# f and g of the next image projected one chunk sooner, F1's moves behind the scores that read it, and another order of V, first tiles and maxima in the prologue

## What is computed

```python
x = x + attention(group_norm(x), Wq, Wk, Wv, gamma)
# attention, with xf of shape (4, 256, 4096):
f = einsum('qc,bcn->bqn', Wq, xf)        # 64 rows
g = einsum('qc,bcn->bqn', Wk, xf)        # 64 rows
h = einsum('vc,bcn->bvn', Wv, xf)        # 256 rows
scores = einsum('bqn,bqm->bnm', f, g)    # 4096 x 4096
beta = softmax(scores, axis=1)           # over n
out = gamma[0] * einsum('bvn,bnm->bvm', h, beta) + xf
```

## Time and profile before

| | |
|---|---|
| median of 3 runs | 1994.29 us |
| the profiled execution: time | 1999.4 us |
| its span, first to last instruction | 1997.6 us |
| mean granted clock of TensorE | 0.987 |
| TensorE busy | 1904.3 us, 95% |
| VectorE busy | 1591.1 us, 80% |
| ScalarE busy | 1574.7 us, 79% |
| GpSimd busy | 1315.6 us, 66% |

### The profile page before, as it was taken

One profiled execution on the slowest core, in us unless ns is written; L12 is line 12 of the kernel. 1 busy time (PEld: TensorE's weight loads), 2 busy tenths in 40 slices (PEclk: granted clock), 3 DMA queues, 4 the chain that ended last, 5 costly groups with the idle time before them and its releaser, 6 DMA issues. The chain is left out here.

```text
span 1997.6 us, 44149 instructions
## 1 busy us (share of the span) xinstructions
PE 1904.3 (95%) x17476; PEld 1568.2 (79%) x17476; DVE 1591.1 (80%) x1931; ACT 1574.7 (79%) x1675; POOL 1315.6 (66%) x760
## 2 busy tenths in 40 slices
PE   4789999999899999999979999999998999999999
PEld 2568888887688888888768888888877888888887
DVE  7678899887568899887756889988765687887784
ACT  4678889887667888988756888888866688888885
POOL 6256668875446766887444676788654477666776
PEclk9899999999899999999989999999999999999999
DMA  4012212211202211211110221122121011111111
GB/s 130 12 33 74 72 31 54 65 33 41 48 21 70 73 46 33 73 51 33 46 35 22 69 73 52 33 65 54 30 54 36 17 33 23 32 31 31 33 28 38
DMA packets 199837, 91.18 MB, mean 46 GB/s; under 512 B 150224, under 2 KB 191440, under 8 KB 199632
## 3 DMA queue, kind: packets, MB, share of 16 engines
q1 hardware_dynamic: 199632, 88.36, 17.0%
HBM read 46.60 MB, written 16.78 MB: 32 GB/s over the span
## 5 line engine op out<-in xcount | busy, mean ns | idle before, releaser
L349 POOL TENSOR_TENSOR PL<-SC,PH 128x1024 f16<-128x1024 f32 x512 | 1090.8, 2136 | 635.6 <-ACT SC L581 631.1
L460 PE MATMUL O<-V,PH 128*128 128x257 f16 x4096 | 1122.1, 274 | 5.6 <-DVE OSB L812 3.1
L462 PE MATMUL O<-V,PL 128*128 128x257 f16 x4096 | 1121.6, 274 | 0.0
L461 PE MATMUL O<-V,PH 128*128 128x256 f16 x4096 | 1120.1, 273 | 0.0
L580 ACT ACTIVATE PH<-SC 128x1024 f16<-128x1024 f32 x512 | 540.3, 1055 | 135.8 <-PE O L462 129.3
L574 ACT ACTIVATE SC<-S 128x1024 f32<-128x1024 f32 x512 | 502.8, 1013 | 157.5 <-issue 98.1
L779 DVE TENSOR_TENSOR SC<-SC,MB 128x1024 f32<-128x1024 f32 x512 | 615.1, 1211 | 0.1
L739 DVE TENSOR_TENSOR XM<-S,XM 128x1024 f32<-128x1024 f32 x384 | 468.4, 1220 | 167.0 <-PE S L448 165.7
L581 ACT ACTIVATE SC<-SC 128x1024 f32<-128x1024 f32 x512 | 534.0, 1043 | 0.0
L460 PEld LDWEIGHTS O<-V,PH 128*128 128x128 f16 x4096 | 407.5, 99 | 55.7 <-DVE OSB L812 4.2
L461 PEld LDWEIGHTS O<-V,PH 128*128 128x128 f16 x4096 | 402.1, 98 | 51.7
(11 more groups left out here) (99 smaller groups left out, 1110.8 us busy)
## 6 DMA issues: line engine op xcount, KB each, us to landing
xin<-x SPq DMA_DIRECT2D x24, 1024.0 KB, 5.8
xres<-x SPq DMA_DIRECT2D x64, 256.0 KB, 2.9
out<-RES SPq DMA_DIRECT2D x64, 256.0 KB, 2.2
ATT<-OT SPq DMA_DIRECT2D x1008, 16.0 KB, 1.9
SC<-x SPq DMA_DIRECT2D x8, 512.0 KB, 8.0
F<-GG SPq DMA_DIRECT2D x64, 64.0 KB, 2.0
GG<-GG SPq DMA_DIRECT2D x32, 128.0 KB, 2.4
SC<-wvT SPq DMA_DIRECT2D x1, 256.0 KB, 6.5
```

The source lines that it names most:

```text
L349: pool.tensor_tensor(PL[:, s % RING, :], sc(s), PH[:, s % RING, :], ALU.subtract).then_inc(pl_ready, 1)
L460: mm(o[:, 0:C + 1], PH[:, n % RING, cols], vh, start=t == 0, stop=False)
L461: mm(o[:, 0:C], PH[:, n % RING, cols], vl, start=False, stop=False)
L462: w = mm(o[:, 0:C + 1], PL[:, n % RING, cols], vh, start=False, stop=t == T - 1)
```

## The change

f and g of the next image are projected in chunk 12 (units 0 to 6) and behind the last step of chunk 13 (unit 7). SyncE moves units 0 to 5 right behind regroup in chunk 13, each pair after the scores of chunk 15 that read it, unit 6 later in that chunk and unit 7 behind regroup in chunk 14. In the prologue, image 0 is loaded in five pieces; GpSimd normalises by multiply and add, once `rbias` is there; V of a unit is projected behind f/g of the unit after it, and from unit 7 on two V stand behind each pair of scores. Step 0's tile is subtracted, exponentiated and weighed in two halves. In chunk 0, ScalarE stores scores ahead of its exponentials, VectorE takes both maxima ahead of subtractions (places in `FIRST_SUB` and `FIRST_EXP`), and the maxima of chunk 1 are shared one step later, in another place than S. The diff, cut:

```diff
-FG_FIRST = CPB - 3
+FG_FIRST = CPB - 4
...
-[(FG_FIRST, g, END) for g in range(7)] + [(FG_FIRST + 1, 0, END)])}
+[(FG_FIRST, g, END) for g in range(7)] + [(FG_FIRST + 1, 7, END)])}
...
+FIRST_SUB = [(3,), (4, 5), (), (), (8,), (9,), (10,), (11,)]
+FIRST_EXP = [(), (3,), (4,), (5,), (6,), (7,), (8,), (9, 10)]
+X0_PIECES = [slice(0, 1024), slice(1024, 2048), slice(2048, 3072), slice(3072, 3584), slice(3584, 4096)]
+VU = NFG - 1
...
 def _(sp):
-    for u in range(NFG):
-        sp.dma_start(x0[:, :, unit(u)], xv[0, :, :, unit(u)]).then_inc(x0_in[u], 16)
+    for i, cols in enumerate(X0_PIECES):
+        sp.dma_start(x0[:, :, cols], xv[0, :, :, cols]).then_inc(x0_in[i], 16)
...
     def move_f(u):
...
+        b, i = divmod(u, NFG)
         f, g = halves(u)
         sp.wait_ge(fg_done, u + 1)
+        if b > 0:
+            sp.wait_ge(s_ready, (b * CPB - 1) * G + i // 2 * 2 + 2)
         sp.dma_start(F1[f, unit(u)], G1[f, unit(u)]).then_inc(f_in[u % NFG], 16)
         sp.dma_start(F1[g, unit(u)], GL[f, unit(u)]).then_inc(f_in[u % NFG], 16)
...
         if k > 0:
             regroup(k - 1)
             if j == FG_FIRST + 1 and b + 1 < BATCH:
-                move_f((b + 2) * NFG - 1)
-                double_g((b + 2) * NFG - 1)
+                for u in range(0, 6, 2):
+                    move_f((b + 1) * NFG + u)
+                    move_f((b + 1) * NFG + u + 1)
+                    if u > 0:
+                        double_g((b + 1) * NFG + u - 2)
+                        double_g((b + 1) * NFG + u - 1)
+            if j == FG_FIRST + 2 and b + 1 < BATCH:
+                move_f((b + 1) * NFG + 7)
             store(k - 1)
...
-            if j == FG_FIRST:
-                for u in range((b + 1) * NFG, (b + 2) * NFG - 1):
-                    move_f(u)
-                    double_g(u)
+            if j == FG_FIRST + 1:
+                move_f((b + 1) * NFG + 6)
+                for u in range(4, 7):
+                    double_g((b + 1) * NFG + u)
+            if j == FG_FIRST + 2:
+                double_g((b + 1) * NFG + 7)
...
-    pool.wait_ge(coefs_ready, 1)
+    pool.wait_ge(res_coefs, 1)
     for u in range(NFG):
         if u >= 2:
             pool.wait_ge(xl_ready[1], u - 1)
-        pool.tensor_scalar(x1n[:, u % 2, :], x0[:, 1, unit(u)], nmean[:, 1:2], nrstd[:, 1:2],
-                           ALU.subtract, ALU.mult).then_inc(x1n_ready, 1)
+        pool.tensor_scalar(x1n[:, u % 2, :], x0[:, 1, unit(u)], nrstd[:, 1:2], rbias[:, 0, 1:2],
+                           ALU.mult, ALU.add).then_inc(x1n_ready, 1)
...
+    for s in range(1, EXP_LEAD):
...
     for n in range(K * G):
...
     for u in range(NFG):
-        if u >= 3:
-            pe.wait_ge(v_done, u - 2)
-        project_fg(u, first_bank(2 * u))
-        if u >= 2:
-            pe.wait_ge(fg_done, u - 1)
-        project_v(u, first_bank(2 * u + 1))
+        if u == 3:
+            pe.wait_ge(fg_done, 1)
+        if u > 3:
+            pe.wait_ge(v_done, u - 3)
+        project_fg(u, first_fg(u))
+        if u > 0:
+            if u > 2:
+                pe.wait_ge(fg_done, u - 1)
+            project_v(u - 1, first_v(u - 1))
...
-    pe.wait_ge(fg_done, NFG)
-    pe.wait_ge(v_done, NFG - 1)
+    pe.wait_ge(fg_done, NFG - 1)
+    pe.wait_ge(v_done, NFG - 3)
     for i in range(G // 2):
...
         scores(2 * i)
-        later_v(NFG + 1 + i)
-    later_v(NFG + 5)
+        later_v(VU + 2 * i)
+        later_v(VU + 2 * i + 1)
     scores(G)
-    later_v(NFG + 6)
+    later_v(NV - 1)
     share_maxima(0, shared0)
-    later_v(NFG + 7)
     scores(G + 2)
...
-        if g == 4 and k + 1 < K:
+        if g == 4 and 0 < k < K - 1:
...
         if q is not None:
...
+        if n == 0:
+            pe.wait_ge(pl_first, 1)
+            for m in range(MB2):
+                pe.wait_ge(v_done, NV - 2 + m)
+                weigh(0, m, range(GT // 2))
         pe.wait_ge(pl_ready, n + 1)
         if g == 0:
             if j == FG_FIRST + 1 and b + 1 < BATCH:
...
             if j == FG_FIRST + 2 and b + 1 < BATCH:
...
         if j == 0:
-            pe.wait_ge(v_done, b * NV + max(2 * g + 2, len(V_AT)) if b else NV)
+            pe.wait_ge(v_done, b * NV + max(2 * g + 2, len(V_AT)) if b else NV - 1 if n == 0 else NV)
...
-        weigh(n, 0)
+        tiles = range(GT) if n > 0 else range(GT // 2, GT)
+        weigh(n, 0, tiles)
         extra(k, g, MID)
-        if g == 3 and k + 1 < K:
-            read = min(n + 2 * G + 1, K * G) if k > 0 else 2 * G
+        if n == 4:
+            share_maxima(1, shared0)
+        if g == 3 and 0 < k < K - 1:
+            read = min(n + 2 * G + 1, K * G)
...
-        weigh(n, 1)
+        weigh(n, 1, tiles)
...
     for i in range(G // 2):
         store(2 * i)
         store(2 * i + 1)
-        later_v(NFG + 1 + i)
-    later_v(NFG + 5)
+        round_v(VU + 2 * i, first_v(VU + 2 * i))
+        round_v(VU + 2 * i + 1, first_v(VU + 2 * i + 1))
...
     store(G)
+    round_v(NV - 1, first_v(NV - 1))
     store(G + 1)
-    later_v(NFG + 6)
-    later_v(NFG + 7)
-    exps(0)
+    act.wait_ge(sub_first, 1)
+    nc.scalar.activation(PH[:, 0, FIRST], sc(0)[:, FIRST], ACT.Exp, bias=SHIFT)
+    nc.scalar.activation(sc(0)[:, FIRST], sc(0)[:, FIRST], ACT.Exp, bias=SHIFT).then_inc(exp_first, 1)
+    act.wait_ge(sub_ready, 1)
+    nc.scalar.activation(PH[:, 0, REST], sc(0)[:, REST], ACT.Exp, bias=SHIFT)
+    nc.scalar.activation(sc(0)[:, REST], sc(0)[:, REST], ACT.Exp, bias=SHIFT).then_inc(exp_done, 1)
+    exps(1)
     store(G + 2)
     store(G + 3)
-    for s in range(1, EXP_LEAD):
-        exps(s)
+    exps(2)
...
     for n in range(K * G):
...
-        if n + EXP_LEAD < K * G:
+        if k > 0 and n + EXP_LEAD < K * G:
...
         if q is not None:
...
+        if k == 0:
+            for s in FIRST_EXP[g]:
+                exps(s)
         extra(k, g, MID)
...
     for i in range(G // 2):
         maximum(2 * i + 1)
         maximum(2 * i)
...
-            later_v(NFG + 1 + i)
+            low_v(VU + 2 * i, first_v(VU + 2 * i))
+            low_v(VU + 2 * i + 1, first_v(VU + 2 * i + 1))
     turn_maxima(0)
     quadrant_maxima(0)
-    later_v(NFG + 4)
-    later_v(NFG + 5)
+    maximum(G + 1)
     column_maxima(0, shared0)
     spread_maxima(0)
-    subtract(0)
-    maximum(G + 1)
-    maximum(G)
-    later_v(NFG + 6)
+    dve.wait_ge(mb_ready, 1)
+    dve.wait_ge(s_stored, 1)
+    for part, done in ((FIRST, sub_first), (REST, sub_ready)):
+        half = sc(0)[:, part].rearrange("p (i m) -> p i m", i=GT // 2)
+        ve.tensor_tensor(half, half, MB[:, 0:M].unsqueeze(1).to_broadcast([P, GT // 2, M]),
+                         ALU.subtract).then_inc(done, 1)
     subtract(1)
-    later_v(NFG + 7)
+    low_v(NV - 3, first_v(NV - 3))
+    low_v(NV - 2, first_v(NV - 2))
     maximum(G + 3)
+    subtract(2)
     maximum(G + 2)
-    for s in range(2, SUB_LEAD):
-        subtract(s)
+    low_v(NV - 1, first_v(NV - 1))
...
     for n in range(K * G):
...
         if q is not None:
             maximum(q + 1)
-        if n + SUB_LEAD < K * G:
+        if k > 0 and n + SUB_LEAD < K * G:
...
         if q is not None:
             maximum(q)
         if n == 2:
             turn_maxima(1)
+            subtract(6)
+            subtract(7)
             quadrant_maxima(1)
+        if n == 4:
+            column_maxima(1, shared0)
+            spread_maxima(1)
+        if k == 0:
+            for s in FIRST_SUB[g]:
+                subtract(s)
...
-        if g == 3 and k + 1 < K:
+        if g == 3 and 0 < k < K - 1:
...
         extra(k, g, MID)
...
```

More of the change, by code:

```diff
@@ L136, in groupnorm_attention @@
         w_in = sem("w_in")
-        x0_in = [sem(f"x0_in{i}") for i in range(NFG)]
+        x0_in = [sem(f"x0_in{i}") for i in range(len(X0_PIECES))]
         xin_in = sem("xin_in")
@@ L174, in groupnorm_attention @@
         pl_ready = sem("pl_ready")
+        sub_first = sem("sub_first")
+        exp_first = sem("exp_first")
+        pl_first = sem("pl_first")
         weighed = sem("weighed")
@@ L199, in first_bank, with first_fg, first_v @@
         def first_bank(i):
-            return O[:, i % 5, :] if i % 5 < OB else S[:, 1, (i % 5 - OB) * 512:(i % 5 - OB + 1) * 512]
+            return O[:, i % 5 - 2, :] if i % 5 >= 2 else S[:, 1, i % 5 * 512:(i % 5 + 1) * 512]
+        def first_fg(u):
+            return first_bank(max(2 * u - 1, 0))
+        def first_v(u):
+            return first_bank(2 * u + 2) if u < VU else O[:, (u + 2) % OB, :]
+        FIRST = slice(0, GW // 2)
+        REST = slice(GW // 2, GW)
         def halves(u):
@@ L374, in low_input @@
                                        ALU.subtract).then_inc(xl_ready[h], 2)
-            for s in range(EXP_LEAD):
+            pool.wait_ge(exp_first, 1)
+            pool.tensor_tensor(PL[:, 0, FIRST], sc(0)[:, FIRST], PH[:, 0, FIRST], ALU.subtract).then_inc(pl_first, 1)
+            pool.wait_ge(exp_done, 1)
```

(37 more changed lines are left out.)

## The result

The changed kernel takes **1938.76 us** (four runs, 1938.01 to 1940.22) against 1994.6 (1993.79 to 1997.14): a ratio of 0.9719, 95% interval 0.9702 to 0.9736, 55.8 us less. The forecast was 1934.2 us, with a range of 1925 to 1949. The profiled execution takes 1938.83, its span is 1937.0.

The account below looks back on a forecast made before the run. TensorE, busy 95% of the span, was taken to bound the kernel, so only its idle and half-clock time could be won. 42.4 + 17.7 = 60.1 us off the median 1994.3 gave 1934.2 us, range 1925 to 1949.

Parts of the forecast that it names:

- Boundaries, 42.4 us: At the three image boundaries: waits and half-clock matmuls go, a gain of 42.4 us, bounds 40.5 and 43.6.
- The wait for unit 7: In chunk 14, the last score group waits for unit 7's move: 0.4 us per boundary, bounds 0 and 0.95.
- Start, 17.7 us: Until all of chunk 0 is weighed: a gain of 17.7 us, bounds 8 and 25.
- the mark: The first score group of chunk 1's loop: moves from 127.17 to 105.5 us.
- Catching up in chunk 1: In chunk 1, after ScalarE's late exponentials in chunk 0: 2 us given back.
- GpSimd's operation: In the projection loop: normalisation by multiply and add takes 1.1 us on 512 columns, 2.08 before.
- The half clock at the first weigh: On both sides of the first weigh, waits of 1 to 2 us like those ending in half clock: 2 us given back.
- The rule against it: GpSimd's normalisation: a port-bound loop gains nothing from exchanged operations; first scores near 51, the sum 5 us smaller.
- I move the median by the same amount: Whole time: the 60.1 us forecast for the profiled execution also comes off the median, 1994.3 to 1934.2.
- B: Start stays bound by its chain, GpSimd no faster or clock low over first tiles: 1944 or 1949 us; chance 0.17.
- C: F1 wait lives on, unit 7's move starting 5 us late at each boundary: 1954 us; chance 0.08.
- E: Slower than before: queue's waits delay store and residual load, holding up GpSimd, then TensorE: over 1994 us; chance 0.02.

Follow-up runs that it names:

- experiment 11: The changed kernel with image 0 loaded in eight pieces again: one execution, 1939.23 us.
- 9: The changed kernel with VectorE's subtractions in groups 5 to 7 of chunk 0 back between the two maxima: one execution, 1943.14 us.
- 10: The changed kernel with the first tile subtracted, exponentiated and weighed whole, not in halves: one execution, 1943.22 us.
- pool_old: The changed kernel with GpSimd's normalisation back to subtract and multiply: 1943.54 us beside 1938.5.
- experiments 1 to 7 and 12: Both kernels unchanged, each part alone, queue-order edits, GpSimd's old normalisation, and the changed kernel with unit 7's move and ScalarE's store earlier: from 1995.44 to 1935.83 us.
- 5: The kernel before with unit 7's move and doubling issued ahead of regroup in chunk 14: 1974.43 us against 1995.8.

## Why the prediction was right, and where it was off

- **What bounds.** Right: idle and half-clock time of TensorE was all there was to win. Most chunks without a projection take 27.42 to 27.46 us in every profile.
- **Boundaries, 42.4 us.** From the head of chunk 12 to that of chunk 15 the three images take 106.5, 107.5 and 107.7 us before and 93.3, 92.9 and 94.1 after: 41.4. Alone the part gave 40.8. The wait for unit 7 was taken at 0.4 and is 0.15, 0 and 1.0. The store and the residual load do wait behind the moves, and cost nothing. One sign was put down wrongly: chunks 13 and 14 together were to take near 65.7 us. They take 56.9, 56.6 and 57.7, since seven of the eight projections are in chunk 12 now; with chunk 12 the forecast comes to 27.4 + 65.7 = 93.1, which fits.
- **Start, 17.7 us.** By the profiles 19.0 at the head of chunk 2, alone 17.8. Four terms were off, and cancelled nearly: the first three follow, the fourth is the half clock. The first scores came 1.0 us sooner than forecast, because the first matmul starts 1.1 sooner: the load was put at 0 (experiment 11 gives it some 0.8, not settled). From the first scores to the mark it takes 60.0 us and not 59.5. Catching up in chunk 1 was put at 2 and costs 3.2. GpSimd's operation was put at 1.1 us from the form on 256 columns and is 0.77; that is worth nothing, since TensorE sets the pace from 2.6 us a unit down (21.2 us from the first matmul to the first scores, 21.1 forecast).
- **The half clock at the first weigh** was put at 2 us and costs at most 0.4. Of the nine profiles with the halved tile four have 15 or 16 of the first tile's 24 matmuls at half clock, three have 4 to 6 and two have none. Yet the first weigh stands 26.4 us behind the first scores in all nine, and the mark 59.65 to 60.07 in all but that of 9. In the second profile of the changed kernel, where the clock stays full (second row in 10), TensorE waits 1.11 us for the maxima of the second group, which then starts only 0.4 us sooner: the half clock is hidden by the wait that was put at 1.6.
- **What is shown of the start by itself.** Of the 22.2 us at the mark 1.1 lie before the first matmul, 6.2 before the first scores (5 of them GpSimd's operation, by pool_old), 5.6 before the first weigh (2.4 the halved tile, by 10) and 9.2 behind it (2.3 VectorE's order in the last three groups, by 9). The rest, some 11 us of V's new places, ScalarE's order and the later hand-over of the maxima, was not taken apart by a run.
- **Slips in the working.** 67.0 + 1.2 + 0.8 is 69.0, not 69.3, and 30.5 + 1.6 + 1.3 is 33.4, not 33.1: the two cancel in 105.5. The first scores before are 4.21, 5.77 and 4.56 us apart, so that no distance is 5.0; the sum taken, 14.1, is near the 14.25 measured after.
- **The rule against it** would have cost 5 us, as pool_old does. The rows were the better guide.
- **The median, the step that was off.** The sum for the profiled execution was 1939.3; it took 1938.83. That is closer than its parts: the boundaries gave 1.0 less than forecast and the start 1.3 more, which is luck. "I move the median by the same amount" was wrong: the median fell by 55.8 us and not by 60.1, and the changed kernel's profiled execution stands at its median, not 5.1 above. The second profile of before shows where most of the 5.1 us were: it is 3.7 us shorter, with TensorE busy 4.1 us less for the same matmuls (1900.2 against 1904.3), 2.4 before the mark and 1.2 in chunks 13 and 14, the very stretches that the change shortens. So the forecast took off time that a median execution had not lost. With that profile (1995.76, and 60.1 - 3.7 taken off) the same sum gives 1939.4. Why the first profile stood so high is open: it lies above all 33 executions of the kernel before that were made beside experiments 1 to 7 and 12 (up to 1998.64), and the one on the chip of experiments 9 to 11 took 1999.46, so that the chip may have a part in it.
- **Rivals.** B came in half: the clock was low at the first weigh, 0.60 from 71 to 74 us, at the start of the stretch that was named as a sign of being wrong, but the time was hidden; GpSimd was faster, and the halved tile kept the wait at 1.06 us. 10 shows what the longer wait would have been like. C was near: unit 7's second transfer is issued at 19.25 us of chunk 14, and the group wants it at 21.2, half a microsecond later than the yardstick, and E's mechanism, a queue that holds GpSimd up, appears in 5 and not here.

## What to carry to other kernels

Where an execution's loss is in waits and in the low clock behind them, compare it with the other executions before subtracting: what is above the median is part of what the change removes, and must not be carried over. A queue that issues in order can hide a needed transfer behind sixteen others; moving it ahead is one line, but whoever waits for the sixteen pays, unless the transfer's input is ready sooner too.

## What was not expected

- On GpSimd a normalisation of 128 x 512 by two per-partition scalars takes 2.08 us with a subtraction in it and 0.77 without, wherever the subtraction stands. From 256 to 512 columns the fast form goes from 0.557 to 0.77 us, less than double.
- One wait of 2.58 us before the first weigh was followed by matmuls at half clock throughout the first tile (0.42 us each for 0.27), and the mark moved 1.1 us more than the first weigh did. Of six profiles with a wait of 1.06 or 1.07 us in the same place four had half clock over 15 or 16 matmuls and two had none, with the same work ahead of it; the mark differs by 0.4 us at most, since TensorE catches up into its next wait.
